# Window attention and a sharpened 1x1 convolution on one core: column halves for 64-wide outputs, the Laplacian on ScalarE and GpSimd, narrower transposes of v, group means later in the opening

## What is computed

```python
x = x + L0(gn(x))      # 8x8 windows, 6 heads of 32: q, k, v by 1x1 convolutions;
                       # o = irfft2(rfft2(q) * rfft2(k)) per channel over the 8x8 window;
                       # attn = softmax(o v^T + position bias); y = attn v; proj(y)
x = x + L1(gn(x))      # out = g + lap(g), lap = 4 g - up - down - left - right, zero padding;
                       # merge: 1x1 convolution 192 -> 192, plus bias
```

## Time and profile before

| | |
|---|---|
| median of 3 runs | 5973.95 us (5973.53 to 5978.52) |
| profiled execution | 5977.56 us |
| its span | 5975.8 us |
| instructions | 206127 |

### The profile page before, as it was taken

The page is one execution under the profiler, slowest core; times in us unless marked ns, Lnnn a source line. Parts: engine busy times, 40 slices in busy tenths (PEclk is TensorE's granted clock), DMA queues, the critical chain, the costliest instruction groups (busy, mean ns, idle before and its releaser), DMA issues.

```text
span 5975.8 us, 206127 instructions
## 1 busy us (share of the span) xinstructions
PE 5684.8 (95%) x91660; PEld 5026.7 (84%) x91660; DVE 5053.2 (85%) x8286; ACT 3167.7 (53%) x6020; POOL 1995.5 (33%) x1286
## 2 busy tenths in 40 slices
PE   7999999999999999999999999999999999999987
PEld 5888888888888888888888888888888888888876
DVE  4777788888889889888888888888888888888876
ACT  2666655555555555555555555555555555555531
POOL 0333333333333333333333333333333333333310
PEclk9999999999999999999999999999999999999999
DMA  4222133323333233332333333333233332222336
GB/s 132 68 63 59 55 79 102 103 79 94 96 106 102 81 92 102 98 99 81 96 102 106 91 82 95 105 104 90 83 101 100 103 85 77 78 78 81 83 90 163
DMA packets 392631, 550.56 MB, mean 92 GB/s; under 512 B 24838, under 2 KB 284873, under 8 KB 391754
## 3 DMA queue, kind: packets, MB, share of 16 engines
q1 hardware_dynamic: 391756, 537.37, 32.1%
HBM read 335.95 MB, written 201.33 MB: 90 GB/s over the span
## 4 chain that ended last, share of the span: by engine, by line
PE 66%; DVE 22%; ACT 9%; issue 2%; DMA 1%; SPq 0%; DVEq 0%
PE b_q L515 20%; PE b_s L621 7%; PE b_t L604 6%; PE b_q L590 5%; PE b_t L580 5%; DVE qkl L907 4%; PE b_s L523 4%; PE b_s L520 3%; ACT qkh L973 3%; PE b_t L562 3%; DVE late L768 2%; PE b_s L466 2%; DVE late L791 2%; DVE ssum L938 2%; ACT probs L1037 2%
## 5 line engine op out<-in xcount | busy, mean ns | idle before, releaser
L1080 POOL TENSOR_TENSOR probs<-probs,srec 128x768 f32<-128x768 f32 x512 | 880.7, 1720 | 2219.5 <-DVE srec L956 2219.5
L1069 POOL TENSOR_TENSOR probs<-probs,smax 128x768 f32<-128x768 f32 x512 | 754.1, 1473 | 1438.3 <-DVE smax L918 1438.3
L973 ACT ACTIVATE vs<-b_q 128x192 f32<-128x192 f32 x1024 | 338.6, 331 | 1360.5 <-PE b_q L515 1360.5
L913 DVE TENSOR_TENSOR probs<-b_s,posb 128x768 f32<-128x768 f32 x512 | 487.9, 953 | 578.5 <-PE b_s L621 578.0
L515 PE MATMUL b_q<-wnh,xh 128*128 128x288 f32 x2048 | 703.3, 343 | 66.7 <-DVE qkl L907 65.4
L907 DVE TENSOR_TENSOR qkl<-b_q,qkh 128x384 fp32r<-128x384 f32 x1024 | 566.0, 553 | 175.5 <-ACT qkh L973 141.3
L523 PEld LDWEIGHTS b_s<-yT,wp 128*128 128x128 f32 x4096 | 618.6, 191 | 53.0
L523 PE MATMUL b_s<-yT,wp 128*128 128x128 f32 x4096 | 622.5, 275 | 0.0
L520 PE MATMUL b_s<-yT,wp 128*128 128x256 f32 x2048 | 613.6, 381 | 2.1 <-DVE probs L913 1.6
L515 PE MATMUL b_q<-wnl,xh 128*128 128x288 f32 x2048 | 606.3, 296 | 0.0
L515 PE MATMUL b_q<-wnh,xl 128*128 128x288 f32 x2048 | 606.1, 296 | 0.0
(11 more groups left out here) (152 smaller groups left out, 13242.6 us busy)
## 6 DMA issues: line engine op xcount, KB each, us to landing
ld<-in_x SPq DMA_DIRECT2D x192, 512.0 KB, 4.9
late<-x_dram SPq DMA_DIRECT2D x112, 640.0 KB, 5.1
xs<-in_x SPq DMA_DIRECT2D x128, 512.0 KB, 5.6
x_dram<-late SPq DMA_DIRECT2D x128, 512.0 KB, 2.8
out<-late SPq DMA_DIRECT2D x128, 512.0 KB
late<-x_dram SPq DMA_DIRECT2D x240, 192.0 KB, 5.7
xs<-in_x SPq DMA_DIRECT2D x128, 256.0 KB, 5.9
x_dram<-late SPq DMA_DIRECT2D x128, 256.0 KB, 3.7
```

What stands on the lines that cost most here:

```text
L913: V.tensor_tensor(scored(i).rearrange("p (t q) m -> p t q m", q=4), scores.rearrange("p (t q m) -> p t q m", q=4, m=N), posb[:, :, :].unsq ...
L973: return A.activation(o, i, ACT.Copy)
L1069: P.tensor_tensor(probs[:, i % 2, :, :], probs[:, i % 2, :, :], smax[:, i % 2, :].unsqueeze(2).broadcast_to([128, 12, N]), ALU.subtract).t ...
L1080: P.tensor_tensor(probs[:, i % 2, :, :], probs[:, i % 2, :, :], srec[:, i % 2, :].unsqueeze(2).broadcast_to([128, 12, N]), ALU.mult).then_ ...
```

## The change

1. Pieces 4 and 5 and the second half of the projection take 64-wide weights, once for output partitions 0 to 63 and once for 64 to 127, each with its own half of the columns; one full-width matmul adds the part of the 64 input channels. The projection's second half thus has 128 columns instead of 256. The weights go from six blocks to five.
2. The Laplacian of a unit: ScalarE writes 5 times the source into z (`centre`), GpSimd makes `diagonal` and subtracts it twice (`neighbours`, half 0 and 1). In the last image's strips VectorE does units 0 and 2 (`late_stencil`), one double after ScalarE's copy.
3. `border` writes the columns in the first three strips of an image only (each buffer once), the row as before.
4. The transposes of v: two of channels 0 to 127, one of channels 64 to 191 of the second pair, and a 64-wide one of channels 128 to 191 of the first, written over the former's upper half. The copy vT has 384 columns. The order of the heads (`HEADS`) is changed to fit, in the weights on the host and in the indices.
5. In the opening the group mean, the spread and the first half of the bias come at m = 56, 58 and 60, the second half after the last position.

```diff
@@ merge_blocks, proj_blocks (both the same)
+    none, square = np.zeros((CB, CA)), np.zeros((CB, CB))
+    corners = np.block([[bb, square], [square, bb]])
+    return np.concatenate([aa, ab, ab, np.concatenate([ba, none]), np.concatenate([none, ba]), corners], axis=1)
@@ piece, p >= 4
-                    mm(o, mats(par, 1), za[:, k, at:at + 256], start=True, stop=False)
-                    mm(o, mats(par, 2), za[:, k, 512 + at:512 + at + 256], start=False, stop=False)
-                    mm(o, mats(par, 5), zb[:, k, at:at + 256], start=False, stop=True).then_inc(m_mm, 1)
+                    for half in range(2):
+                        out_rows = slice(half * CB, (half + 1) * CB)
+                        mm(o[out_rows], mats(par, 1)[:, out_rows], za[:, k, half * 512 + at:half * 512 + at + 256],
+                           start=True, stop=False, skip_group_check=True)
+                    mm(o, mats(par, 4), zb[:, k, at:at + 256], start=False, stop=True,
+                       skip_group_check=True).then_inc(m_mm, 1)
@@ second half of the projection
+            def project_b():
+                o = b_r[:, 256:384]
+                for i in range(2):
+                    out_rows = slice(i * CB, (i + 1) * CB)
+                    mm(o[out_rows], wp[:, 1, out_rows], yT[:, i, :, :].rearrange("p w (r c) -> p r w c", c=WS),
+                       start=True, stop=False, skip_group_check=True)
+                mm(o, wp[:, 4, :], rest, start=False, stop=True, skip_group_check=True).then_inc(proj_mm, 1)
@@ transposes of v
                     for i in range(2):
-                        for t in range(2):
-                            last = nc.tensor.transpose(vt_out[:, i, t, :],
-                                                       vs[:, (2 * j + i) % 8, t * N:t * N + 128], ident[:, :])
-                    last.then_inc(vT_mm, 1)
+                        nc.tensor.transpose(vt_out[:, i, :], vs[:, at + i, 0:CA], ident[:, :])
+                    nc.tensor.transpose(vt_out[:, 2, :], vs[:, at + 1, CB:C], ident[:, :])
+                    nc.tensor.transpose(vt_out[0:CB, 2, :], vs[:, at, CA:C], ident[:, :]).then_inc(vT_mm, 1)
@@ opening
-                if m == 8:
+                if m == 56:
                     group_mean(0)
-                elif m == 16:
+                elif m == 58:
                     group_spread(0)
-                elif m == 40:
+                elif m == 60:
                     bias(0, 0)
-                elif m == 52:
-                    pe.wait_ge(m_read, 3)
-                    bias(0, 1)
...
             last.then_inc(pos_mm, 1)
+            pe.wait_ge(m_read, 3)
+            bias(0, 1)
@@ which unit, and by whom
+        def stencil_unit(j):
+            blk, ph = divmod(2 * j, 8)
+            v = blk - STENCIL_LAG
+            return (v, ph // 2) if 0 <= v < STRIPS and ph < 6 else None
+        LATE = STRIPS - NS
+        def by_vector(v, unit):
+            return v >= LATE and unit != 1
@@ VectorE: border, then the late units (edges is gone)
             def border(v):
                 s = v % NS
+                if 3 <= s < NS - 1:
+                    return
...
+            def late_stencil(v, unit):
...
+                V.tensor_tensor(d, src[:, r + 1:r + 6, 0:W + 1], src[:, r:r + 5, 1:W + 2], ALU.add).then_inc(late_diag, 1)
+                dve.wait_ge(late_diag, n)
+                dve.wait_ge(five_done, 3 * v + unit + 1)
+                V.tensor_tensor(zz, zz, d[:, 0:4, 0:W], ALU.subtract).then_inc(late_nb, 1)
+                dve.wait_ge(late_nb, n)
+                V.tensor_tensor(zz, zz, d[:, 1:5, 1:W + 1], ALU.subtract).then_inc(late_z, 1)
@@ VectorE, main loop
                 m_result(2 * j)
-                edges(2 * j)
                 norms(2 * j)
+                unit = stencil_unit(j - 1)
+                if unit and by_vector(*unit):
+                    late_stencil(*unit)
                 if pair(0):
                     remainders(2 * j + 1)
-                edges(2 * j + 1)
@@ ScalarE, main loop, between the copies of osb and qh
+                if stencil_unit(j):
+                    centre(*stencil_unit(j))
@@ GpSimd, main loop
             for j, pair in doubles():
+                unit = stencil_unit(j - 1)
+                if unit and by_vector(*unit):
+                    unit = None
+                if unit:
+                    diagonal(*unit)
+                    neighbours(*unit, 0)
...
                     P.tensor_tensor(tokens(xl, 0, h), windows(0, h), tokens(xh, 0, h).bitcast(F32), ALU.subtract
                                     ).then_inc(xl_done, 1)
+                if unit:
+                    neighbours(*unit, 1)
```

More of the change, by code:

```diff
@@ L270, in program @@
             a_count[it] = a_count[it - 1] + (m_task(it) is not None and by_act)
+        border_count = list(itertools.accumulate(int(v % NS < 3 or v % NS == NS - 1) for v in range(STRIPS)))
         def m_region(it):
@@ L467, in piece @@
                     at = p % 2 * 256
-                    last = mm(o, mats(par, 3 + p // 2), zb[:, k, at:at + 256], start=False, stop=not alone)
+                    last = mm(o, mats(par, 2 + p // 2), zb[:, k, at:at + 256], start=False, stop=not alone)
                     if alone:
@@ L567, in _ @@
                 if pair(4):
-                    project(b_r[:, 256:512], 3).then_inc(proj_mm, 1)
+                    project_b()
                 m_slot(2 * j + 1, pair)
@@ L581, in _ @@
                                           vs[rows, (2 * k + i) % 8, h * HD:(h + 1) * HD],
-                                          probsT[rows, i, h, :], start=True, stop=True)
+                                          probsT[rows, i, HEADS.index(h), :], start=True, stop=True)
                     last.then_inc(y_mm, 1)
@@ L1064, in _, with diagonal, neighbours @@
             P.memset(ones[:, :], 1.0).then_inc(ones_done, 1)
-            for j, pair in doubles():
+            d = dg[:, :].rearrange("p (r c) -> p r c", c=W + 1)
+            def diagonal(v, unit):
+                src, r, _ = unit_views(v, unit)
+                if unit == 0 or v >= LATE:
+                    pool.wait_ge(border_w, border_count[v])
+                    pool.wait_ge(src_in[v % 3], 48 * (v // 3 + 1))
+                pool.wait_ge(z_done, pool_units(v, unit) - 1)
+                P.tensor_tensor(d, src[:, r + 1:r + 6, 0:W + 1], src[:, r:r + 5, 1:W + 2], ALU.add
+                                ).then_inc(diag_done, 1)
+            def neighbours(v, unit, half):
+                _, _, zz = unit_views(v, unit)
+                n = pool_units(v, unit)
+                if half == 0:
+                    pool.wait_ge(diag_done, n)
+                    pool.wait_ge(five_done, 3 * v + unit + 1)
+                    P.tensor_tensor(zz, zz, d[:, 0:4, 0:W], ALU.subtract).then_inc(nb_done, 1)
+                else:
+                    pool.wait_ge(nb_done, n)
+                    P.tensor_tensor(zz, zz, d[:, 1:5, 1:W + 1], ALU.subtract).then_inc(z_done, 1)
+            for j, pair in doubles():
+                unit = stencil_unit(j - 1)
[4 more added lines that the diff above has]
+                    neighbours(*unit, 0)
                 if pair(2):
@@ L1090 @@
     x = a["x"]
+    qk = np.concatenate([part * C + h * HD + np.arange(HD) for part in range(2) for h in HEADS])
     arrays = {
         "x": x,
-        "wqkvT": np.concatenate([a["L0_conv_QK_w"], a["L0_conv_V_w"]]).T,
-        "qkvb": np.concatenate([a["L0_conv_QK_b"], a["L0_conv_V_b"]])[None],
+        "wqkvT": np.concatenate([a["L0_conv_QK_w"][qk], a["L0_conv_V_w"]]).T,
+        "qkvb": np.concatenate([a["L0_conv_QK_b"][qk], a["L0_conv_V_b"]])[None],
         "proj": proj_blocks(a["L0_conv_proj_w"]),
```

158 lines of the change are left out of this document (70 added, 88 removed).

## The result

The changed kernel takes 5897.42 us (median of 4 runs, 5897.16 to 5900.44) against 5973.74 us (4 runs, 5969.49 to 5978.52): a ratio of 0.9874, 95% interval 0.9858 to 0.9889. That is 76 us less; the forecast was 203 us less. The time lies inside the range, but only 38% of the forecast gain came. The range had been stretched to take in rival A and most of D, and neither of them came, so that the time lies in it is no success of the sum.

The account below looks back on a forecast made before the run. TensorE, busy 95%, was taken as the bound, with about 160 us of stalls behind VectorE and GpSimd. Stalls -130, halves -73, opening -4, tail +4 gave -203 us: 5770 us, range 5690 to 5960 us.

Parts of the forecast that it names:

- rival A: The narrow transpose of v changes the array's shape, some 175 us more: 5945 us; chance 0.25.
- D: The stalls stay behind another wait, or halves run one by one: +130 to +200, 5900 to 5970 us; chance 0.11.
- the stalls: TensorE waits for VectorE's last result and, at strip heads, the position-bias add; moving Laplacian and borders off VectorE: -130 us.
- The balance that gave 160 us: Over the attention: 5430 us of strips against 5636, less 40 us for weights and statistics, leaves about 160 us of stalls.
- the lock: VectorE and GpSimd take a shared port pair exclusively per instruction; expected at xhl and borders, up to 1.5 us each.
- Tail: Strips at the end: 10.69 us instead of 10.45, unit 2 behind piece 5's result: +4 us; bounds -25 and +8.
- Column halves: On TensorE, project_b and pieces 4 and 5 each 0.10 us shorter, double without pieces about the same: -73 us.
- the excursion: On TensorE, entering and leaving a smaller array shape: 0.20 us back, 0.09 in, some 0.04 first narrow load, 0.33 us.
- Narrower transposes: Transposes of v on TensorE: the 64-wide one keeps the old price of 0.12 us, so no change in the sum.
- Opening: Before the first qkv: group mean issued later, bias 0 at 78.5 us, qkv at 91.5 to 92: gain 3.6 us.
- B: Array shape changes cost nothing inside full-width work, so the halves give 273 us instead of 73: 5570 us; chance 0.07.
- C: GpSimd becomes the loop, deciding near 2.15 us per new operation; at 2.5 us each 6000 us, slower; chance 0.12.

Follow-up runs that it names:

- laplace_only: The kernel before with only the Laplacian moved to ScalarE and GpSimd (VectorE in late strips) and the shorter border: 5936.74 us, ratio 0.9938.
- halves_two_parts: The kernel before with the column halves, the projection's result added in two operations instead of three (some output values differ): 5954.77 us, ratio 0.9967.
- halves_only: The kernel before with the column halves alone, the projection's result added in three operations: 6028.21 us, ratio 1.0091.
- both_vector_tail: The changed kernel, GpSimd's unit after chores in three doubles per image, source loaded earlier, tail reordered, VectorE making all late units, earlier copy: 5794.52 us, ratio 0.9704.

## Why the prediction was wrong, step by step

The forecast sum was -130 - 73 - 4 + 4 = -203 us. The traces give -70 - 40 - 3 + 36 = -77.

- **"Of some 160 us I take 130 us back", the stalls.** The step that failed most, by 60 us. The mechanism was right where it was read: both stalls are gone in ordinary strips (44.13 to 42.97 us with the Laplacian alone). But it was read in one strip and spread over all. The balance that gave 160 us put the weights and statistics at 40 us; in the table strips 1, 2, 13 and 14 of the kernel before lie 11.5 us per image above an ordinary strip, some 80 us in seven images, so that about 125 us of stalls were there. In strips 2 and 13 VectorE's chores meet two new operations of GpSimd ahead of the subtraction: 1.1 + 3.0 us lost where 1.15 each was to be gained, 6.4 us per image or some 45 us of the 60. The experiment that takes them from under three doubles per image gives 35 us back. The other 16 us or so: strips 0, 3, 14 and 15 had less stall to lose (-0.5 to -0.65 us each). The prediction named the lock but placed it only at xhl and the borders; "early in the double" is where `root`, the casts and the add stand.
- **Tail, "+0.24 us x 17 = +4 us", bounds -25 and +8.** Measured +36. The order was right, unit 2 behind the result of piece 5, but it was priced at undisturbed durations: GpSimd's unit stands beside it, and the wait became 3.48 us, a strip of 11.31 us at full clock instead of 10.69, against 10.45 before: (11.31 - 10.45) x 17 = 15 us. The clock, which the sum did not contain, adds more: 12.9 us on average, 1.6 x 17 = 27 us. The two make 42 and not 36 us, since the tail of before lost some us to the clock too, two strips of 12.13 us among them.
- **Column halves, -73 us.** Mechanism and prices right: pairs at once, 0.79 us for `project_b` against 0.77 forecast; the double of pieces 4 and 5 went from 11.64 to 11.37 us. The sum came to -40 with the transposes. It lacked the third operation of VectorE, 0.22 us per double: hidden in ordinary strips of the changed kernel, and by itself enough to turn the halves into a loss where VectorE sets the pace. Against `laplace_only` an ordinary strip gained 0.46 us, but strips 1, 2, 3, 4 and 13 together nothing, 2.3 us per image or some 16 us; that the third operation does this beside the chores fits, but no run separates it. And in the double without pieces (9.77 us before, 9.76 after) nothing was gained, where 0.11 us was counted. The tail's clock is a cost of the halves too: 20 us in the kernel before, and here 4 to 7 us, 272.6 us with the Laplacian alone against 277.0 to 280.1 in the four kernels with the changed kernel's tail. (The 0.04 us that the excursion had for the first narrow load stands in no row.)
- **Narrower transposes, 0.** Right; rival A is out: L588 takes 0.11 us. (Its price was 512 x 0.33 = 169 us by its own terms, not 175.)
- **Opening, -4 us.** Right: `bias` 0 at 79.00 us (78.5 forecast), first qkv at 91.96. Over all traces the first qkv starts at 93.2 to 96.2 us with the old opening and at 90.9 to 92.3 with the new one.
- **Rivals.** B is out, the shape's price is there. C is out for ordinary doubles: GpSimd's operations take 1599, 1193 and 1194 ns, below the 2.15 us from which it would decide; at the 2.5 us for which it named 6000 us, its own terms give 0.62 + 0.7 us of 327 doubles above 5770, some 6200. D is out: no wait stood right behind. What came was none of them: the lock, at places that the prediction did not look at.

Open: what makes the granted clock of a tail strip full or lower, and so why `halves_two_parts` had seven strips at full clock and `halves_only` none; and what `both_vector_tail` would gain without the earlier copy.

## What to carry to other kernels

A stall priced in one period must be priced in every kind of period: list the periods that carry extra work before multiplying by their number. An engine that is given work is not only busy longer; it slows its neighbour at every point where they overlap, so move such work away from the neighbour's short chained operations, and price what sharing really leaves: in the tail 5.2 us for one unit beside GpSimd against 4.5 us for two alone. And look at both ends of a producer's change: a cheaper matmul that leaves its result in one more part costs the engine that reads it.

## What was not expected of the hardware

- Two-column products of VectorE took 1.50 us beside a GpSimd operation of 1.58 us and 0.16 us without. The 512-column ones took 1.55 beside it, 0.69 alone. Adds that read their scores from PSUM did not change (0.96 us).
- With much the same wait per strip, TensorE's granted clock was lower in one tail with pieces 4 and 5 in halves than with full width: 0.83 to 0.90 at 2.52 us of wait, and 0.94 to 1.00 at 2.43 us. In the former some four pairs of a strip's matmuls came 0.85 us apart instead of 0.43, the lower level of 1.2 GHz, in the first half of the strip. The same halves and wait in `halves_two_parts` had 1.00 for seven strips, so the form makes it likelier and does not decide it.
- Taking GpSimd's share of the Laplacian over to VectorE did not lengthen VectorE's ring in the tail, it shortened it by some 0.6 us per strip; the strip went from 10.3 to 8.6 us, most of it by the earlier copy made in the same run.
